# A layer kernel on one core: the inverse root of the gated norm moves from VectorE (a seed and three Newton steps) to one GpSimd power

## The chip, the cores and the metric

The kernel runs on one core of one Trainium2 chip. The metric is the device time of one launch in microseconds (us); the median of several runs counts. In the text TensorE is also called PE, VectorE DVE, ScalarE ACT, GpSimd POOL and SyncE SP, as the profile does.

## The reference

`x` is 4 x 512 x 256, that is 16 tiles of 128 tokens. Cut to what matters:

```
xn = (x - mean) / sqrt(var + 1e-5)
q, k, v = silu(xn Wq), silu(xn Wk), silu(xn Wv)         # 16 heads of 16
o  = chunked linear attention with decay, a state per head carried from chunk to chunk
o  = o * sigmoid((xn Wg1) Wg2)
og = o.reshape(b, n, 16, 16)
og = og * rsqrt(mean(og * og, axis=-1) + 1e-5)          # one factor per token and head
s  = (og * norm_w) Wo
g  = silu(quantised(xn) @ quantised(W2))                # through float8
out = x + s * g
```

The line with `rsqrt` is what the change touches: for one tile it is a table of 128 tokens x 16 heads.

## The kernel before

The program is written out by hand, with a semaphore for nearly every buffer. Each engine runs the same software pipeline over the 16 tiles: a step (i, j) works on tile n = 4i + j, prepares tile n+1 (projections, transposes) and tile n+2 (layer norm), finishes the norm and the transposed output of tile n-1, and the output projection and the sum with x of tile n-2. Steps 0 and 1 stand alone, steps 2 to 13 are a loop of three rounds with four steps in each, and steps 14 to 17 stand alone again: 16 has no tile n of its own any more, 17 only closes. Each engine takes its instructions in the order in which the program has them, so the order in `step` of each engine sets everything.

The parts that the change and the prediction touch, by engine:

- DVE: `gate_o` (L747) makes `og` = (tanh + 1) * o, which is twice the gated o; ACT `square_o` (L566) squares it; `sum_heads` (L753) sums 16 values of each head into `og_sum`, 128 x 16. `rsqrt` (L766 to L776) then makes `og_rs` in twelve small steps on 128 x 16, each of which waits for the one before over the semaphore `s_rs`: variance, shift right by one, seed from the constant 0x5F3759DF, and three times the three Newton instructions. In `step` they are spread by `newton(a, b)` between the other work of the engine.
- POOL: `norm_factor` (L336, L338) adds epsilon and takes the power -0.5 of a 128 x 1 column for the layer norm; `round_y` (L345, L348) and `put_nan` (L354) belong to the quantisation; `spread_state` (L375) writes the masked state, once or twice in a step; `add_x` (L392) makes `y` of tile n-2; `decay_k` (L361) makes `kd` of tile n+1; `head_norm` (L384) makes `on` = og * og_rs of tile n-1.
- PE: `transpose_o` (L1172) transposes `on`; it stands in the row just ahead of `add_chunk` (L1160), which completes `ps_o` of tile n, from which the next `gate_o` reads. `gate` (L1067) of the next step waits until `og` is made.
- DVE at a step's end: `decay_q` (L740), `exponent` (L688, which waits for ACT `e_y`, L561), `magic` (L692), `gate_o` (L747), `low_oT` (L782).
- The last tiles: in step 15 there is no tile to prepare, in step 16 `head_norm_last` on DVE (L793) takes the place of POOL's `head_norm`, and PE fills its wait with six matmul pairs of `keep_warm` (L1187).

Of the kernel before, what the change touches and what calls it, by code (L numbers as in the profile page):

```python
# [8 lines left out]
I32 = mybir.dt.int32  # L9
# [8 lines left out]
def layer_kernel(nc, x, log_decay, Wq, Wk, Wv, Wo, Wg1, Wg2, norm_w, W2, scale, scale1, out):  # L18
# [25 lines left out]
    LOOPS = B - 1  # L44
    RS_STEPS = 12
    WO_LOADS = 16 * (1 + KH)
# [6 lines left out]
    with ExitStack() as ctx:  # L53
# [90 lines left out]
        og_rs = sb("og_rs", [P, H])  # L144
        og_y2 = sb("og_y2", [P, H])
        og_half = sb("og_half", [P, H])
        on = sb("on", [P, D])
# [180 lines left out]
        def _(pool):  # L328
# [36 lines left out]
            def spread_state(i, j, c):  # L365


                if j % NB == NB - 1 and c == 1:
# [9 lines left out]
                                ALU.mult).then_inc(s_sx, 1)  # L378

            def head_norm(i, j):  # L380

                pool.wait_ge(s_rs, RS_STEPS * (num(i, j) + 1))
                need(pool, s_oTps, num(i, j))
                g.tensor_tensor(on[:].rearrange("p (h e) -> p h e", h=H), og[:].rearrange("p (h e) -> p h e", h=H),  # L384
                                og_rs[:].unsqueeze(2).broadcast_to([P, H, E]), ALU.mult).then_inc(s_on, 1)
# [64 lines left out]
            def step(pool, i, j):  # L450
# [10 lines left out]
                if cur:  # L461
                    spread_state(i, j, 0)

                if known(i, j - 2) and known(i, j - 1):
# [188 lines left out]
        def _(dve):  # L653
# [100 lines left out]

            def rsqrt(i, j, first, last):

                for m in range(first, last):
                    if m == 0:  # L760
                        dve.wait_ge(s_sum, num(i, j) + 1)
                        need(dve, s_on, num(i, j))
                    else:
                        dve.wait_ge(s_rs, RS_STEPS * num(i, j) + m)
                    if m == 0:
                        ins = v.tensor_scalar(og_var[:], og_sum[:], 1.0 / E, 4.0 * EPS, ALU.mult, ALU.add)  # L766
                    elif m == 1:
                        ins = v.tensor_scalar(og_half[:].bitcast(I32), og_var[:].bitcast(I32), 1, None, ALU.logical_shift_right)
                    elif m == 2:
                        ins = v.tensor_scalar(og_rs[:].bitcast(I32), og_half[:].bitcast(I32), -1.0, float(0x5F3759DF), ALU.mult, ALU.add)  # L770
                    elif m % 3 == 0:
                        ins = v.tensor_tensor(og_y2[:], og_rs[:], og_rs[:], ALU.mult)  # L772
                    elif m % 3 == 1:
                        ins = v.scalar_tensor_tensor(out=og_half[:], in0=og_y2[:], scalar=-0.5, in1=og_var[:], op0=ALU.mult, op1=ALU.mult)  # L774
                    else:
                        ins = v.scalar_tensor_tensor(out=og_rs[:], in0=og_half[:], scalar=1.5, in1=og_rs[:], op0=ALU.add, op1=ALU.mult)  # L776
                    ins.then_inc(s_rs, 1)

# [113 lines left out]
            def step(dve, i, j):  # L892
# [3 lines left out]

                def newton(a0, b0):
                    if back:
                        rsqrt(i, j - 1, a0, b0)

                if not cur:

                    if back:
                        sum_heads(i, j - 1)
                        newton(0, 8)
                    else:
                        dve.wait_ge(s_y, G - 1)
                    product(i, j - 2)
                    if back:
                        newton(8, RS_STEPS)  # L910
                        head_norm_last(i, j - 1)
                        low_oT(i, j - 1)
                    else:
                        add_x_last(i, j - 2)
                    return
                if not nxt:

                    mask(i, j, 0)
                    mask(i, j, 1)
                    add_state(i, j, 0)  # L920
                    mask(i, j, 2)
                    mask(i, j, 3)
                    sum_heads(i, j - 1)
                    newton(0, 2)
                    product(i, j - 2)
                    newton(2, RS_STEPS)
                    gate_o(i, j)
                    low_oT(i, j - 1)
                    return
# [14 lines left out]
                if first:  # L944
# [4 lines left out]
                    finish_w2()  # L949
                newton(0, 1)  # L950
                if nxt:
                    find_nan(i, j + 1)
                newton(1, 2)
                if known(i, j - 2):
                    product(i, j - 2)
                newton(2, 4)
                if norm and not first:
                    shift_x(i, j + 2)
                newton(4, 5)
                if cur and not first:  # L960
                    add_state(i, j, 0)
                newton(5, 6)
                if first:
                    scale_wo()
                if cur:
                    mask(i, j, 2)
                newton(6, 8)
                if cur:
                    mask(i, j, 3)
                newton(8, 9)  # L970
                if cur:
                    add_state(i, j, 1)
                newton(9, 10)
                if nxt:
                    low_g1(i, j + 1)
                newton(10, RS_STEPS)
                if norm:
# [317 lines left out]
```

## Time and profile before

| | us |
|---|---|
| median of three runs | 188.94 (188.51 to 189.07) |
| the profiled execution: its own time | 189.03 |
| its span, first to last instruction | 187.1 |
| PE busy | 166.7 (89% of the span) |
| DVE busy | 147.3 (79%) |
| POOL busy | 104.6 (56%) |
| ACT busy | 103.1 (55%) |

The profile is of one execution. The span leaves out 1.9 us at the edges of the execution. Busy times of the engines lie beside each other; which of them sets the end is read from the chain of waits, not from the shares. Rows of the trace give a start in us from the beginning of the span, a duration and the instruction, as out<-in; the shape is partitions x columns.

### The profile page before, as it was taken

The numbers are of one execution on the slowest core, as the hardware profiler recorded it, in microseconds if no ns is written. First come the engines' busy times: TensorE is split into PE (matmuls) and PEld (weight loads), VectorE is DVE, ScalarE is ACT, GpSimd is POOL, SyncE is SP. The second block draws the span as 40 slices with busy tenths as digits, with TensorE's granted clock in tenths as the row PEclk, the third lists the DMA queues.
The fourth block names the chain that finished last, engine by engine and source line by source line (L and its number), as shares of the span: only waits on it lengthen the run. The fifth ranks groups of instructions, "written<-read, shape, count | busy, mean of one in ns | idle before, by whom it ended". The sixth has DMA issues, their size and how long they took to land.

```text
span 187.1 us, 7410 instructions
## 1 busy us (share of the span) xinstructions
PE 166.7 (89%) x2510; PEld 127.1 (68%) x2510; DVE 147.3 (79%) x548; ACT 103.1 (55%) x283; POOL 104.6 (56%) x180
## 2 busy tenths in 40 slices
PE   4868469999999999999999999999999999998392
PEld 4745248677777777777777777777777777776181
DVE  1789985979797979888888879797979697857672
ACT  3584446483839383847575665748483847372100
POOL 6654871747565666656574656575747474732210
PEclk9999966999999999999999999999999999999657
DMA  5295300000100010000000000000000000010000
GB/s 145 71 254 166 112 5 0 4 4 4 33 0 32 0 33 4 30 4 28 0 28 0 28 0 27 1 0 28 0 28 0 28 0 28 0 33 4 28 28 28
DMA packets 7201, 5.82 MB, mean 31 GB/s; under 512 B 1744, under 2 KB 7184, under 8 KB 7184
## 3 DMA queue, kind: packets, MB, share of 16 engines
q1 hardware_dynamic: 7184, 5.60, 9.9%
q8 instruction: 10, 0.16, 0.4%
q14 instruction: 7, 0.06, 0.1%
HBM read 3.50 MB, written 2.10 MB: 30 GB/s over the span
## 4 chain that ended last, share of the span: by engine, by line
PE 61%; DVE 12%; ACT 11%; issue 8%; POOL 3%; DMA 3%; SPq 1%; ACTq 0%; DVEq 0%; POOLq 0%
PE b_scores L1081 11%; PE b_xo L1180 8%; PE b_att L1107 5%; PE b_kv L1028 4%; PE b_kv L1033 3%; PE b_kv L1030 3%; PE b_qg L1028 3%; ACT qT L526 3%; PE b_scores L1124 3%; PE b_gate L1067 3%; ACT ffn_silu L509 2%; DVE og L747 2%; ACT e_y L561 2%; PE b_att L1143 2%; PE b_qg L1033 2%
## 5 line engine op out<-in xcount | busy, mean ns | idle before, releaser
L1081 PE MATMUL b_scores<-qT,kT 32*64 32x128 f32 x512 | 31.6, 283 | 1.5 <-DVE probs L717 1.2
L717 DVE TENSOR_TENSOR probs<-b_scores,decay_mask 128x256 f32<-128x256 f32 x64 | 26.6, 418 | 2.6 <-PE b_scores L1081 2.3
L1081 PEld LDWEIGHTS b_scores<-qT,kT 32*64 32x64 f32 x512 | 20.1, 132 | 12.2 <-issue 8.9
L545 ACT ACTIVATE xn<-x_sb,shift,rstd 128x256 f32 (+1 forms) x15 | 9.0, 602 | 35.1 <-DVE shift L681 35.1
L375 POOL TENSOR_TENSOR state_c<-state,own_head 128x256 f32<-128x256 f32 x28 | 20.7, 738 | 11.3 <-DVE state L733 10.2
L345 POOL TENSOR_TENSOR e_sum<-e_y,e_magic 128x256 f32<-128x256 f32 x16 | 11.7, 729 | 25.0 <-DVE e_magic L692 25.0
L384 POOL TENSOR_TENSOR on<-og,og_rs 128x256 f32<-128x256 f32 x15 | 9.3, 622 | 17.3 <-DVE og_rs L776 15.5
L774 DVE SCALAR_TENSOR_TENSOR og_half<-og_y,og_var 128x16 f32<-128x16 f32 x48 | 14.7, 306 | 0.7
L392 POOL TENSOR_TENSOR y<-sg,x_sb 128x256 f32<-128x256 f32 x15 | 11.0, 731 | 6.1 <-DVE sg L787 6.1
L772 DVE TENSOR_TENSOR og_y<-og_rs 128x16 f32<-128x16 f32 x48 | 13.7, 285 | 0.8
L1124 PE MATMUL b_scores<-probs,v_parity 64*32 64x64 f32 x1024 | 14.0, 229 | 0.2 <-DVE probs L717 0.2
L1124 PEld LDWEIGHTS b_scores<-probs,v_parity 64*32 64x32 f32 x1024 | 11.4, 108 | 3.8 <-issue 3.3
L526 ACT ACTIVATE qT<-b_qk,head_parity 128x256 f32<-128x256 f32 x32 | 13.4, 474 | 0.0
L740 DVE TENSOR_TENSOR qdT<-b_qk,q_decay 128x256 f32<-128x256 f32 x16 | 6.8, 424 | 8.2 <-ACT qT L526 8.2
L1107 PE MATMUL b_att<-kv,kd 64*64 64x64 f32 x224 | 12.8, 234 | 0.0
L348 POOL TENSOR_TENSOR e_q<-e_sum,e_magic 128x256 bf16<-128x256 f32 x16 | 12.1, 754 | 1.3
L681 DVE SCALAR_TENSOR_TENSOR shift<-mean_var,rstd 128x1 f32<-128x1 f32 x16 | 10.5, 658 | 1.8 <-POOL rstd L338 0.8
L733 DVE SCALAR_TENSOR_TENSOR state<-state,chunk_decay,b_att 128x64 f32<-128x64 f32 x48 | 11.2, 273 | 0.9 <-issue 0.5
L688 DVE TENSOR_SCALAR e_exp<-e_y 128x256 int32<-128x256 int32 x16 | 4.7, 292 | 9.1 <-ACT e_y L561 9.1
L1107 PEld LDWEIGHTS b_att<-kv,kd 64*64 64x64 f32 x224 | 8.9, 136 | 4.3 <-issue 2.2
L354 POOL TENSOR_TENSOR xq<-e_q,e_nan 128x256 bf16<-128x256 bf16 x16 | 10.8, 674 | 1.7 <-DVE e_nan L698 1.7
L1187 PE MATMUL b_scores<-ident 128*128 128x128 f32 x46 | 9.5, 386 | 2.5 <-POOL ident L403 2.5
(135 smaller groups left out, 458.7 us busy)
## 6 DMA issues: line engine op xcount, KB each, us to landing
out_dram<-y SPq DMA_DIRECT2D x16, 128.0 KB, 1.7
x_sb<-in_L_attn_x_dram SPq DMA_DIRECT2D x3, 512.0 KB, 3.5
x_sb<-in_L_attn_x_dram SPq DMA_DIRECT2D x1, 384.0 KB, 5.4
w_f<-in_L_attn_Wk_dram SPq DMA_DIRECT2D x1, 256.0 KB, 2.9
w_f<-in_L_attn_Wv_dram SPq DMA_DIRECT2D x1, 256.0 KB, 3.1
w_f<-in_L_attn_Wq_dram SPq DMA_DIRECT2D x1, 256.0 KB, 3.4
w_f<-in_L_ffn_input_dram SPq DMA_DIRECT2D x1, 256.0 KB, 4.1
wo_f<-in_L_attn_Wo_dram SPq DMA_DIRECT2D x1, 256.0 KB, 3.9
```

The costliest lines, as they stand in the source:

```text
L345: g.tensor_tensor(e4_sum[:], e4_y[:], e4_magic[:], ALU.add).then_inc(s_e4p, 1)
L348: g.tensor_tensor(e4_q[:], e4_sum[:], e4_magic[:], ALU.subtract).then_inc(s_e4p, 1)
L375: g.tensor_tensor(dst[:].rearrange("p k (b c) -> p k b c", b=2), state[:].unsqueeze(2).broadcast_to([P, KH, 2, C]), own_head[:].rearrange( ...
L526: a.activation(qT[:, u, :, par, :], ps_qT, ACT.Copy, scale=head_parity[:, par:par + 1]).then_inc(s_qkT, 1)
L717: v.tensor_tensor(probs[:, r], b_score[r % 2][:, 0:4 * C].rearrange("p (i c) -> p i c", i=4), decay_mask[:, r], ALU.mult).then_inc(s_probs, 1)
L772: ins = v.tensor_tensor(og_y2[:], og_rs[:], og_rs[:], ALU.mult)
L774: ins = v.scalar_tensor_tensor(out=og_half[:], in0=og_y2[:], scalar=-0.5, in1=og_var[:], op0=ALU.mult, op1=ALU.mult)
L1028: t.matmul(dst, xT_hi[:, kk], w_hi[:, kk, a:b], start=(kk == 0), stop=False)
L1081: mm = t.matmul(b_score[r % 2][c * C:c * C + C, half * 2 * C:(half + 1) * 2 * C], kT[rows, u, half, c * C:c * C + C], qT[rows, u, half, :, ...
L1107: mm = t.matmul(ps_state[b * C:b * C + C, half, :], kd[rows, u, cols], kv[rows, u, D + cols.start:D + cols.stop], start=True, stop=True)
L1124: mm = t.matmul(ps_avT[32 * r:32 * r + 32, half, c, :], v_parity[rows, u, par * D + half * P + 32 * r:par * D + half * P + 32 * r + 32], p ...
L1180: mm = t.matmul(ps_out, lhs[:, kk], rhs[:, kk], start=(n == 0 and kk == 0), stop=(n == 2 and kk == KH - 1))
```

## The change

`rsqrt` goes. What is left of it on DVE is `head_var`, the first of the twelve instructions (variance, scaled and with epsilon). POOL gets `head_rsqrt`: one `tensor_tensor` with the operation power, variance to the exponent -0.5, on 128 x 16, with its result in `og_rs`. It stands behind the first `spread_state` of the step and ahead of `add_x`. In step 16, where `head_norm_last` runs on DVE, the power is on POOL all the same. The semaphore `s_rs` counts two steps for each tile in place of twelve.

```diff
@@ -42,7 +42,7 @@
     Q0 = 2 * D
     NW = 3 * D + GR
     LOOPS = B - 1
-    RS_STEPS = 12
+    RS_STEPS = 2
     WO_LOADS = 16 * (1 + KH)
     assert (P, NB, KH, HH, E, GR) == (128, 4, 2, 8, 16, 16)
 
@@ -142,8 +142,6 @@
         og_sum = sb("og_sum", [P, H])
         og_var = sb("og_var", [P, H])
         og_rs = sb("og_rs", [P, H])
-        og_y2 = sb("og_y2", [P, H])
-        og_half = sb("og_half", [P, H])
         on = sb("on", [P, D])
         oT_hi = sb("oT_hi", [P, KH, P], F32R)
         oT_lo = sb("oT_lo", [P, KH, P], F32R)
@@ -377,6 +375,11 @@
                                 own_head[:].rearrange("p (b c) -> p b c", b=2).unsqueeze(1).broadcast_to([P, KH, 2, C]),
                                 ALU.mult).then_inc(s_sx, 1)
 
+            def head_rsqrt(i, j):
+                pool.wait_ge(s_rs, RS_STEPS * num(i, j) + 1)
+                need(pool, s_on, num(i, j))
+                g.tensor_tensor(og_rs[:], og_var[:], minus_half[:], ALU.pow).then_inc(s_rs, 1)
+
             def head_norm(i, j):
 
                 pool.wait_ge(s_rs, RS_STEPS * (num(i, j) + 1))
@@ -460,7 +463,8 @@
                     put_nan(i, j + 1)
                 if cur:
                     spread_state(i, j, 0)
-
+                if known(i, j - 1):
+                    head_rsqrt(i, j - 1)
                 if known(i, j - 2) and known(i, j - 1):
                     add_x(i, j - 2)
                 if nxt:
@@ -752,29 +756,10 @@
                 need(dve, s_rs, RS_STEPS * num(i, j))
                 v.tensor_reduce(og_sum[:], og_sq[:].rearrange("p (h e) -> p h e", h=H), AX_X, ALU.add).then_inc(s_sum, 1)
 
-            def rsqrt(i, j, first, last):
-
-
-
-                for m in range(first, last):
-                    if m == 0:
-                        dve.wait_ge(s_sum, num(i, j) + 1)
-                        need(dve, s_on, num(i, j))
-                    else:
-                        dve.wait_ge(s_rs, RS_STEPS * num(i, j) + m)
-                    if m == 0:
-                        ins = v.tensor_scalar(og_var[:], og_sum[:], 1.0 / E, 4.0 * EPS, ALU.mult, ALU.add)
-                    elif m == 1:
-                        ins = v.tensor_scalar(og_half[:].bitcast(I32), og_var[:].bitcast(I32), 1, None, ALU.logical_shift_right)
-                    elif m == 2:
-                        ins = v.tensor_scalar(og_rs[:].bitcast(I32), og_half[:].bitcast(I32), -1.0, float(0x5F3759DF), ALU.mult, ALU.add)
-                    elif m % 3 == 0:
-                        ins = v.tensor_tensor(og_y2[:], og_rs[:], og_rs[:], ALU.mult)
-                    elif m % 3 == 1:
-                        ins = v.scalar_tensor_tensor(out=og_half[:], in0=og_y2[:], scalar=-0.5, in1=og_var[:], op0=ALU.mult, op1=ALU.mult)
-                    else:
-                        ins = v.scalar_tensor_tensor(out=og_rs[:], in0=og_half[:], scalar=1.5, in1=og_rs[:], op0=ALU.add, op1=ALU.mult)
-                    ins.then_inc(s_rs, 1)
+            def head_var(i, j):
+
+                dve.wait_ge(s_sum, num(i, j) + 1)
+                v.tensor_scalar(og_var[:], og_sum[:], 1.0 / E, 4.0 * EPS, ALU.mult, ALU.add).then_inc(s_rs, 1)
 
             def low_oT(i, j):
                 dve.wait_ge(s_oThi, num(i, j) + 1)
@@ -894,20 +879,15 @@
                 back = known(i, j - 1)
                 first = isinstance(i, int) and num(i, j) == 0
 
-                def newton(a0, b0):
-                    if back:
-                        rsqrt(i, j - 1, a0, b0)
-
                 if not cur:
 
                     if back:
                         sum_heads(i, j - 1)
-                        newton(0, 8)
+                        head_var(i, j - 1)
                     else:
                         dve.wait_ge(s_y, G - 1)
                     product(i, j - 2)
                     if back:
-                        newton(8, RS_STEPS)
                         head_norm_last(i, j - 1)
                         low_oT(i, j - 1)
                     else:
@@ -921,9 +901,8 @@
                     mask(i, j, 2)
                     mask(i, j, 3)
                     sum_heads(i, j - 1)
-                    newton(0, 2)
+                    head_var(i, j - 1)
                     product(i, j - 2)
-                    newton(2, RS_STEPS)
                     gate_o(i, j)
                     low_oT(i, j - 1)
                     return
@@ -947,33 +926,26 @@
                     magic(0, 1)
                     add_state(0, 0, 0)
                     finish_w2()
-                newton(0, 1)
+                if back:
+                    head_var(i, j - 1)
                 if nxt:
                     find_nan(i, j + 1)
-                newton(1, 2)
                 if known(i, j - 2):
                     product(i, j - 2)
-                newton(2, 4)
                 if norm and not first:
                     shift_x(i, j + 2)
-                newton(4, 5)
                 if cur and not first:
                     add_state(i, j, 0)
-                newton(5, 6)
                 if first:
                     scale_wo()
                 if cur:
                     mask(i, j, 2)
-                newton(6, 8)
                 if cur:
                     mask(i, j, 3)
-                newton(8, 9)
                 if cur:
                     add_state(i, j, 1)
-                newton(9, 10)
                 if nxt:
                     low_g1(i, j + 1)
-                newton(10, RS_STEPS)
                 if norm:
                     low_xT(i, j + 2)
                 if first:
```

What it does to the order on VectorE, from the variance of tile n-1 (`og_var`) to the first update of the state, in a step of the loop. Before:

```order
L766 TENSOR_SCALAR og_var<-og_sum 128x16
L696 REGISTER_ALU
L698 TENSOR_SCALAR e_nan<-e_q 128x256
L764 REGISTER_ALU
L768 TENSOR_SCALAR og_half<-og_var 128x16
L787 TENSOR_TENSOR sg<-b_xo,ffn_silu 128x256
L764 REGISTER_ALU
L770 TENSOR_SCALAR og_rs<-og_half 128x16
L764 REGISTER_ALU
L772 TENSOR_TENSOR og_y<-og_rs 128x16
L681 SCALAR_TENSOR_TENSOR shift<-mean_var,rstd 128x1
L764 REGISTER_ALU
```

and now, up to the update of the state:

```order
L762 TENSOR_SCALAR og_var<-og_sum 128x16
L700 REGISTER_ALU
L702 TENSOR_SCALAR e_nan<-e_q 128x256
L772 TENSOR_TENSOR sg<-b_xo,ffn_silu 128x256
L685 SCALAR_TENSOR_TENSOR shift<-mean_var,rstd 128x1
L728 ISA
L734 ISA
L737 SCALAR_TENSOR_TENSOR state<-state,chunk_decay,b_att 128x64 x2
```

The variance keeps its place; all that belonged to the seed and to the Newton steps is gone, here and further down the step.

On GpSimd, from the quantised x of tile n+1 (`xq`) over the spread state (`state_c`) to the normed output of tile n-1 (`on`), in the same step. Before:

```order
L354 TENSOR_TENSOR xq<-e_q,e_nan 128x256
L371 ISA
L375 TENSOR_TENSOR state_c<-state,own_head 128x256
L388 REGISTER_ALU
L390 ISA
L392 ISA
L392 TENSOR_TENSOR y<-sg,x_sb 128x256
L361 TENSOR_TENSOR kd<-kv,k_decay 128x256
L382 REGISTER_ALU
L384 TENSOR_TENSOR on<-og,og_rs 128x256
```

and now:

```order
L352 TENSOR_TENSOR xq<-e_q,e_nan 128x256
L369 ISA
L373 TENSOR_TENSOR state_c<-state,own_head 128x256
L379 ISA
L381 TENSOR_TENSOR og_rs<-og_var,minus_half 128x16
L393 ISA
L395 ISA
L395 TENSOR_TENSOR y<-sg,x_sb 128x256
L359 TENSOR_TENSOR kd<-kv,k_decay 128x256
L385 REGISTER_ALU
L387 TENSOR_TENSOR on<-og,og_rs 128x256
```

One instruction more stands between `state_c` and `y`, and `y`, `kd` and `on` all stand behind it.

## Rows read from the trace of the kernel before

**Rows 1.** The page's slices: TensorE's granted clock, 40 equal slices, in tenths

```profile
PEclk9999966999999999999999999999999999999657
```

**Rows 2.** Two steps: length, busy us of PE, PEld, DVE, ACT, POOL, granted clock

```profile
51.69:61.10 9.41, 9.18 (x157) 6.99 (x152) 7.96 (x32) 6.03 (x17) 5.48 (x9) 1.00 0.05 16
80.77:90.56 9.79, 9.79 (x170) 7.54 (x169) 8.31 (x34) 6.02 (x17) 6.16 (x10) 1.00 0.04 13
```

**Rows 3.** Waits over the whole span; us in total, times, longest

```profile
POOL on L384 <- DVE og_rs L776: 15.5, 14, 1.6
```

**Rows 4.** The chain of waits at a step's end; start us, us, what

```profile
89.53 0.41 ACT e_y L561
...
89.95 0.30 DVE e_exp L688
...
90.56 0.43 DVE og L747
...
91.08 0.36 PE b_gate L1067
```

**Rows 5.** Timeline of GpSimd in that step; start us, us, instruction, idle before

```profile
85.08 0.74 POOL L375 TENSOR_TENSOR state_c<-state,own_head 128x256 f32<-128x256 f32 x1 [0.56 <-DVE state L733]
85.78 0.73 POOL L392 TENSOR_TENSOR y<-sg,x_sb 128x256 f32<-128x256 f32 x1
86.46 0.63 POOL L361 TENSOR_TENSOR kd<-kv,k_decay 128x256 f32<-128x256 f32 x1
88.08 0.62 POOL L384 TENSOR_TENSOR on<-og,og_rs 128x256 f32<-128x256 f32 x1 [0.99 <-DVE og_rs L776]
88.66 0.74 POOL L375 TENSOR_TENSOR state_c<-state,own_head 128x256 f32<-128x256 f32 x1
```

**Rows 6.** Lines L338 (power) and L336 (sum) of GpSimd; durations ns min/median/max

```profile
L338 POOL TENSOR_TENSOR rstd<-var_eps,minus_half x16: 550/552/836, 3.9 to 151.2; 128x1 f32<-128x1 f32 x16
...
L336 POOL TENSOR_TENSOR var_eps<-mean_var,eps_col x16: 191/192/372, 3.6 to 150.9; 128x1 f32<-128x1 f32 x16
```

**Rows 7.** Groups of VectorE that the change removes; busy us, mean ns, idle before

```profile
L774 DVE SCALAR_TENSOR_TENSOR og_half<-og_y,og_var 128x16 f32<-128x16 f32 x48 | 14.7, 306 | 0.7
L772 DVE TENSOR_TENSOR og_y<-og_rs 128x16 f32<-128x16 f32 x48 | 13.7, 285 | 0.8
L776 DVE SCALAR_TENSOR_TENSOR og_rs<-og_half,og_rs 128x16 f32<-128x16 f32 x48 | 9.0, 188 | 0.7
L768 DVE TENSOR_SCALAR og_half<-og_var 128x16 int32<-128x16 int32 x16 | 3.1, 191 | 0.1
L770 DVE TENSOR_SCALAR og_rs<-og_half 128x16 int32<-128x16 int32 x16 | 2.7, 166 | 0.1
```

**Rows 8.** Timeline of TensorE at the end of that step

```profile
89.25 0.44 PE L1172 MATMUL b_xo<-ident,on 128*128 128x128 f32 x2
89.52 0.61 PE L1160 MATMUL b_att<-ident,avT 128*128 128x128 f32 x4
```

**Rows 9.** Timeline of VectorE at that step's start

```profile
80.77 0.41 DVE L747 SCALAR_TENSOR_TENSOR og<-gate_tanh,b_att 128x256 f32<-128x256 f32 x1
```

**Rows 10.** Timeline of all engines in step 15, tile 14's norm

```profile
171.94 0.17 DVE L766 TENSOR_SCALAR og_var<-og_sum 128x16 f32<-128x16 f32 x1
...
172.73 0.72 POOL L392 TENSOR_TENSOR y<-sg,x_sb 128x256 f32<-128x256 f32 x1 [2.11 <-DVE sg L787]
172.77 0.72 DVE L772 TENSOR_TENSOR og_y<-og_rs 128x16 f32<-128x16 f32 x1
...
172.96 0.71 PE L1160 MATMUL b_att<-ident,avT 128*128 128x128 f32 x4 [0.47 <-ACT avT L571]
...
174.98 0.17 DVE L776 SCALAR_TENSOR_TENSOR og_rs<-og_half,og_rs 128x16 f32<-128x16 f32 x1
175.23 0.62 POOL L384 TENSOR_TENSOR on<-og,og_rs 128x256 f32<-128x256 f32 x1 [1.78 <-DMA out_dram<-y]
...
175.91 0.69 PE L1172 MATMUL b_xo<-ident,on 128*128 128x128 f32 x2 [2.23 <-POOL on L384]
```

## Prediction

> **What bounds the kernel now.** I read in this order: the busy times by stretch, the chain of waits, the timeline of each engine over one step, the waits in total, and then the last steps alone.
>
> The windows show two steps of the loop, each from one `gate_o` to the next: 9.79 us where the state is updated twice, 9.41 us in every fourth step, where it is updated once [rows 2]. PE is busy for 9.79 of 9.79 and 9.18 of 9.41 us, DVE for 8.31, POOL for 6.16. The granted clock is 1.00, the upper of the two levels, 2.4 GHz. So PE is all but full. The chain shows what closes the loop beside it: ACT makes `e_y`, DVE `e_exp`, the magic number and `og`, and then PE goes on with the gate matmul L1067 [rows 4]. `e_exp` starts when `e_y` is there, so DVE stands idle ahead of it however little it had to do before. None of the Newton instructions is in that chain. They end in `og_rs`, for which POOL's `on` waits, 14 times, 15.5 us in all [rows 3]; but `on` ends at 88.70 [rows 5] and PE takes it at 89.25, behind other matmuls [rows 8]. That wait is POOL's and costs nothing as long as `on` is there by then.
>
> **What is removed.** 176 instructions on DVE: three groups of 48 with 14.7, 13.7 and 9.0 us, and two of 16 with 3.1 and 2.7 us, together 43.2 us of busy time, 2.7 us for each of 16 tiles [rows 7]. In the loop I cost this at nothing: what DVE hands to PE and ACT next hangs on `e_y` [rows 4], and PE is full [rows 2]. What comes instead when it goes is a longer idle time ahead of `e_exp`.
>
> **What is added.** 16 powers of 128 x 16 on POOL, one for a tile. They stand ahead of `y`, `kd` and `on` of the same step, so each of these is later by the length D of the power, less the wait of `on`, which now follows `kd` at once.
>
> D is in no row. The nearest is the power of 128 x 1, 552 ns, and beside it the sum of 128 x 1, 192 ns [rows 6]. `y`, a sum of 128 x 256, takes 0.73 us [rows 5], so a column of a plain operation costs (730 - 192) / 255 = 2.1 ns. The power of one column costs 360 ns more than its sum. If all of this is paid once an instruction, D = 552 + 15 x 2 = 0.58 us. If it is paid again for each column, D = 192 + 16 x 360 = 5.95 us. The two ends are a factor of ten apart. Halfway by ratio is 1.86 us, halfway by difference 3.3 us. The row that D is nearest to is the 128 x 1 power itself, and it stands at the lower end, so I take little above the ratio's middle: 2.1 us, which is 0.10 us for each further column, under a third of the 0.36 us.
>
> The Trainium skill (GPSIMD Engine Reference, Performance pitfalls for Q7 kernels) says that a chain of dependent fp32 operations on these cores pays 4 cycles an operation unless independent work is interleaved. The 360 ns for one column agree with a long chain of that sort; by the rule without interleaving D is at its upper end, with it near the lower, and no row of the trace tells which. The sum would be that of the second or of the first rival below.
>
> **What D does to a step.** I lay the power into the step from 80.77 to 90.56. `state_c` starts at 85.08, and the power takes the place of `y` at 85.78 [rows 5]. Then `y` starts at 85.78 + D, `kd` 0.68 us later, `on` 0.65 us after that, at 87.11 + D, and it ends at 87.73 + D. PE wants it at 89.25 [rows 8], so up to D = 1.5 us nothing is late.
>
> Behind that, two loops form, and the longer sets the step:
> - `og` 80.77 [rows 9], then `on` at 87.73 + D, the transpose L1172 0.04 us later, L1160 0.27 us after it, 0.61 us long [rows 8], and the next `og` 0.05 us later, at 88.70 + D. The step is 7.93 + D. It passes 9.79 at D = 1.86 and 9.41 at D = 1.48.
> - In steps with two updates the second `state_c` starts 0.58 us after `on` starts and takes 0.74 us [rows 5]: it ends at 88.43 + D. If `e_exp` can't run beside it, the next `og` comes 0.61 us later [rows 4], at 89.04 + D, and the step is 8.27 + D, longer than 9.79 from D = 1.52.
>
> Whether the second loop is real hangs on one thing. In step 15 the Newton product `og_y` on 128 x 16 took 0.72 us, from 172.77 to the end of POOL's `y` [rows 10], while its group has a mean of 285 ns [rows 7]: DVE stood still while POOL ran. I take the mean of both loops. The Trainium skill (SBUF — State Buffer, SBUF: two separate sides) says that GpSimd and VectorE share one pair of ports as a lock held for a whole instruction, and that a VectorE operation with two inputs from SBUF, or in a two-port mode, waits for it; the rows on `og_y` agree. By it the power keeps such instructions off for all of D, and the second loop is the one that counts.
>
> With D = 2.1 us the loops give 10.03 and 10.37 us. For the ten steps of tiles 2 to 14 with two updates that is 0.24 to 0.58 us over 9.79, mean 0.41, so 4.1 us; for the three with one update 10.03 - 9.41 = 0.62, so 1.9 us. Step 1 has no `y` ahead of `on` and stays. Together +6.0 us.
>
> **The end.** In step 15 nothing else covers the Newton steps. `og_var` of tile 14 ends at 172.11, the last Newton step at 175.15, and `on` starts at 175.23; PE waits for it for 2.23 us, though it was free from 173.67 on [rows 10]. Afterwards the power runs at about 172.15, `y` behind it for 0.69 us, and `on` starts at 172.84 + D: earlier by 2.39 - D, with D = 2.1 by 0.3 us. In step 16 the power is beside the matmuls of `keep_warm`, which I cost at nothing; it costs what D is longer than the eleven Newton instructions that it replaces there.
>
> **Sum.** 189.03 + 6.0 - 0.3 = 194.7 us for an execution like the profiled one. That is 0.09 above the median before, which gives 194.6; I say 194.7.
>
> **The rivals.**
> - *The power is cheap* (D from 0.58 to 1.5 us). For it: every other POOL instruction grows by only 2.1 ns a column. Against it: the power is the one whose first column costs 360 ns. Nothing is late in the loop, and the end gains 2.39 - D: with D = 1.0 us 1.4 us, so 187.5 us; from 1.8 to 0.9 us over the case. If the shorter wait also keeps the clock up, of which the page shows 0.6, 0.5 and 0.7 in the last three slices [rows 1], it is up to 1.5 us more. This is the case on the other side. It decides below D = 1.5 us, and its price is only the end.
> - *The power is paid in full for each column* (D from 3.6 to 5.95 us). With D = 4.0 the loops give 11.93 and 12.27: 10 x 2.31 + 3 x 2.52 = 30.7, and 1.6 later at the end, so 221 us; with 5.95 about 249. Against it: sixteen columns would have to share nothing. PE would then stand idle for over 2 us in each step, and after the 2.23 us wait in step 15 the clock fell [rows 1, 10], which would add to it.
> - *The relief of VectorE counts* after all: 2.7 us a tile less on an engine that is busy for 8.31 of 9.79 us. Against it stands the idle time that already lies ahead of `e_exp`. The only gap on PE is 0.23 us, in the steps of 9.41 us [rows 2], so at most 3 x 0.23 = 0.7 us and the end: 186.9 us.
>
> **Chances.** Middle power, D from 1.5 to 3.6 us, own range 189 (D = 1.6) to 215 us: 0.44, and the forecast 194.7. Full price: 0.18. Cheap: 0.34. Relief: 0.04. A difference under 0.3%, 0.57 us, is what a measurement of this kernel can't tell; it takes in D from about 1.55 to 1.7 us and the cheap case's upper edge, 0.08. So faster 0.35, same 0.08, slower 0.57. The range from 187.0 to 222 leaves out D above 4.1 us and the best of the cheap case.
>
> **What would show it.** The duration of `og_rs` on POOL is the first number to read. If D is near 2.1 us, PE shows a wait ahead of L1172 for `on` of some tenths of a us in nearly every step, the steps are 10.0 to 10.4 us long, and `on` follows `kd` without idle time. If D is under 1.5 us, the steps stay at 9.79 and 9.41, DVE's idle time ahead of `e_exp` grows, and the only change is ahead of L1172 in step 15. The forecast is wrong if D is outside 1.5 to 3.6 us, or if the steps don't follow 7.93 + D to 8.27 + D. If `e_exp` starts with the end of the second `state_c`, the second loop is right; if the two overlap, the first.

## The result, and the profile after

| | before | after |
|---|---|---|
| median, us | 188.72 (188.14 to 189.07, 4 runs) | 203.94 (203.36 to 204.63, 4 runs) |
| span of the profiled execution, us | 187.1 | 202.9 |
| PE busy, us (share) | 166.7 (89%) | 171.2 (84%) |
| DVE busy | 147.3 (79%) | 123.3 (61%) |
| POOL busy | 104.6 (56%) | 150.6 (74%) |

The ratio is 1.078 (95% interval 1.0737 to 1.0823): 15 us slower, forecast 6 us slower. DVE lost 24 us of busy time and POOL gained 46 us. The 43.2 us of the removed groups [rows 7] shrink to 24 mainly because their records partly overlap those of DVE's other work (with each stretch counted once they fill 28.5 us alone), and because `e_exp` and the magic number take 5.4 us more in all.

Two groups of the page after, and its slices of the clock (columns: busy us, mean ns | idle before, releaser):

```profile
L381 POOL TENSOR_TENSOR og_rs<-og_var,minus_half 128x16 f32<-128x16 f32 x16 | 46.7, 2917 | 3.8 <-DVE og_var L762 3.8
L1144 PE MATMUL b_xo<-ident,on 128*128 128x128 f32 x32 | 7.3, 310 | 15.3 <-POOL on L387 15.0
...
PEclk9999756999999999999699999999999969999757
```

The power takes 2.92 us, not 2.1. PE now waits for `on` ahead of its transposes, 15.0 us in all; before, it did so only at the end. The slices of the clock dip twice within the loop as well, where before [rows 1] those of the loop all stood at 9.

The waits say the same from both sides; `on`, for which POOL waited 15.5 us before [rows 3], now never waits:

```profile
PE b_xo L1144 <- POOL on L387: 15.0, 12, 2.8
...
DVE on L778 <- POOL og_rs L381: 1.4, 1, 1.4
```

Two steps of the loop, from one `gate_o` to the next (the columns of [rows 2]):

```profile
86.32:97.07 10.75, 9.61 (x157) 7.33 (x156) 7.24 (x22) 6.13 (x17) 9.06 (x12) 1.00 0.04 13
97.07:108.19 11.12, 11.12 (x163) 8.77 (x164) 5.84 (x21) 6.41 (x18) 8.29 (x10) 0.85 0.03 12
```

Where [rows 2] had 9.79 us with PE busy throughout, there are 10.75 us with 9.61 busy. In the second step the clock was on its lower level from 98.4 to about 101.8; PE had been busy since 96.15, the end of a wait of 1.14 us.

The same step on POOL and PE, to be laid beside [rows 5] and [rows 8]:

```profile
90.61 0.74 POOL L373 TENSOR_TENSOR state_c<-state,own_head 128x256 f32<-128x256 f32 x1 [0.47 <-DVE state L737]
91.31 2.92 POOL L381 TENSOR_TENSOR og_rs<-og_var,minus_half 128x16 f32<-128x16 f32 x1
94.20 0.73 POOL L395 TENSOR_TENSOR y<-sg,x_sb 128x256 f32<-128x256 f32 x1
94.89 0.62 POOL L359 TENSOR_TENSOR kd<-kv,k_decay 128x256 f32<-128x256 f32 x1
95.47 0.62 POOL L387 TENSOR_TENSOR on<-og,og_rs 128x256 f32<-128x256 f32 x1
...
96.15 0.44 PE L1144 MATMUL b_xo<-ident,on 128*128 128x128 f32 x2 [1.14 <-POOL on L387]
```

From `state_c` to the end of `on` POOL works without a gap, and PE starts 0.06 us after `on` ends.

Where the 15.8 us of span went, by the starts of `og` in the two timelines: the start of tile 0 is later by 0.17; from tile 0 to 1 the step grew from 9.02 to 10.38, 1.36; from tile 1 to 14 from 126.13 to 139.51, 13.38; from tile 14 to the end from 19.13 to 20.02, 0.89.

### The profile page after: what moved, and what is told of

Read it like the earlier page. It is cut to its first block, busy times and chain, and to the rows that moved or that the text cites. A ratio compares the mean times of both kernels' runs of the same rounds, so it can differ in the third digit from the quotient of the medians.

```text
span 202.9 us, 7112 instructions
## 1 busy us (share of the span) xinstructions
PE 171.2 (84%) x2510; PEld 130.3 (64%) x2510; DVE 123.3 (61%) x372; ACT 104.2 (51%) x283; POOL 150.6 (74%) x196
## 4 chain that ended last, share of the span: by engine, by line
issue 32%; PE 19%; POOL 18%; DVE 6%; ACT 3%; POOLq 1%; DVEq 1%; ACTq 0%
POOL og_rs L381 4%; POOL xq L352 4%; POOL on L387 4%; PE b_scores L1053 3%; POOL kd L359 3%; PE b_xo L1144 3%; PE b_xo L1152 2%; PE b_att L1132 2%; POOL y L395 2%; DVE og L751 1%; POOL state_c L373 1%; DVE probs L721 1%; PE b_kv L1002 1%; PE b_kv L1000 1%; POOL var_eps L334 1%
## 5 line engine op out<-in xcount | busy, mean ns | idle before, releaser
L381 POOL TENSOR_TENSOR og_rs<-og_var,minus_half 128x16 f32<-128x16 f32 x16 | 46.7, 2917 | 3.8 <-DVE og_var L762 3.8
L1053 PE MATMUL b_scores<-qT,kT 32*64 32x128 f32 x512 | 31.7, 283 | 1.1 <-DVE probs L721 1.1
L343 POOL TENSOR_TENSOR e_sum<-e_y,e_magic 128x256 f32<-128x256 f32 x16 | 11.6, 728 | 11.7 <-DVE e_magic L696 11.7
L1144 PE MATMUL b_xo<-ident,on 128*128 128x128 f32 x32 | 7.3, 310 | 15.3 <-POOL on L387 15.0
L541 ACT ACTIVATE oT_hi<-b_xo 128x256 fp32r<-128x256 f32 x16 | 6.2, 386 | 20.5 <-PE b_xo L1144 20.5
L1144 PEld LDWEIGHTS b_xo<-ident,on 128*128 128x128 f32 x32 | 3.3, 145 | 19.0 <-POOL on L387 18.3
L334 POOL TENSOR_TENSOR var_eps<-mean_var,eps_col 128x1 f32<-128x1 f32 x16 | 3.2, 203 | 15.1 <-DVE mean_var L677 15.1
L685 DVE SCALAR_TENSOR_TENSOR shift<-mean_var,rstd 128x1 f32<-128x1 f32 x16 | 9.5, 592 | 6.0 <-POOL rstd L336 3.3
L1000 PE MATMUL b_kv<-w_hi,xT_hi 128*128 128x512 f32 x32 | 11.1, 431 | 1.8 <-ACT xT_hi L488 1.8
L692 DVE TENSOR_SCALAR e_exp<-e_y 128x256 int32<-128x256 int32 x16 | 6.4, 403 | 9.1 <-ACT e_y L565 9.1
```

Of the source, the lines that this page charges most:

```text
L343: g.tensor_tensor(e4_sum[:], e4_y[:], e4_magic[:], ALU.add).then_inc(s_e4p, 1)
L381: g.tensor_tensor(og_rs[:], og_var[:], minus_half[:], ALU.pow).then_inc(s_rs, 1)
L1000: t.matmul(dst, xT_hi[:, kk], w_hi[:, kk, a:b], start=(kk == 0), stop=False)
L1053: mm = t.matmul(b_score[r % 2][c * C:c * C + C, half * 2 * C:(half + 1) * 2 * C], kT[rows, u, half, c * C:c * C + C], qT[rows, u, half, :, ...
L1144: mm = t.transpose(ps_oT[:, kk, :], on[:, kk * P:kk * P + P], ident[:])
```

## The experiments

**e1: what a power costs.** `for w in (1, 2, 4, 8, 16, 32, 64): tensor_tensor(out, base[:, 0:w], exponent[:, 0:w], pow)` (shortened), two further powers of 16 columns (bases of 1.0; 16 partitions only) and two products, behind GpSimd's last work in the kernel before.

> The kernel before, with a row of GpSimd operations put behind its last one: powers -0.5 of 1, 2, 4, 8, 16, 32 and 64 columns on 128 partitions, then 16 columns with all bases 1.0, 16 columns on 16 partitions only, and as a yardstick plain products of 16 and 64 columns. Its time isn't the question (a few us longer), the durations are. Theory (the power pays per column beyond its first): from 0.55 us for one column and 2.92 for sixteen, (2.92 - 0.55)/15 = 0.158 us a column, so 0.71, 1.02, 1.66, 2.92, 5.4 and 10.5 us. Rival A (the 2.92 us in the changed kernel are mostly a wait for a port that VectorE holds): here VectorE is idle or nearly so, and sixteen columns take well under 2.9 us. Rival B (cost in blocks, a fixed price up to 16 columns): 2 to 16 columns all near 2.9 us. If bases of 1.0 are quicker the data decide, and if 16 partitions are quicker the cores' number of lanes does; the theory expects the same 2.92 us for both.

Groups of POOL with shapes kept apart (columns as in [rows 7]):

```profile
L481 POOL TENSOR_TENSOR sweep_out<-lag_decay,sweep_exp 128x64 f32<-128x64 f32 x1 | 10.5, 10542 | 0.0
L481 POOL TENSOR_TENSOR sweep_out<-lag_decay,sweep_exp 128x32 f32<-128x32 f32 x1 | 5.4, 5422 | 0.0
L481 POOL TENSOR_TENSOR sweep_out<-lag_decay,sweep_exp 128x16 f32<-128x16 f32 x1 | 2.9, 2896 | 0.0
L483 POOL TENSOR_TENSOR sweep_out<-ones_row,sweep_exp 128x16 f32<-128x16 f32 x1 | 2.9, 2895 | 0.0
L485 POOL TENSOR_TENSOR sweep_out<-lag_decay,sweep_exp 16x16 f32<-16x16 f32 x1 | 2.9, 2890 | 0.0
...
L481 POOL TENSOR_TENSOR sweep_out<-lag_decay,sweep_exp 128x8 f32<-128x8 f32 x1 | 1.6, 1632 | 0.0
...
L481 POOL TENSOR_TENSOR sweep_out<-lag_decay,sweep_exp 128x4 f32<-128x4 f32 x1 | 1.0, 1009 | 0.0
...
L481 POOL TENSOR_TENSOR sweep_out<-lag_decay,sweep_exp 128x2 f32<-128x2 f32 x1 | 0.7, 733 | 0.0
L481 POOL TENSOR_TENSOR sweep_out<-lag_decay,sweep_exp 128x1 f32<-128x1 f32 x1 | 0.5, 549 | 0.1
...
L487 POOL TENSOR_TENSOR sweep_out<-lag_decay,sweep_exp 128x16 f32<-128x16 f32 x1 | 0.2, 210 | 0.0
```

The price is a straight line: (10542 - 549) / 63 = 159 ns a column, neither the 2 ns nor the 360 ns of the two bounds. Sixteen columns take the same with an idle VectorE (it had no work from 186.42 us on), with bases of 1.0 and on 16 partitions, and shorter powers are cheaper, so rivals A and B fall. The time, 212.22 us in the one run, is the added work.

**e2: a product in place of the power.**

```diff
-g.tensor_tensor(og_rs[:], og_var[:], minus_half[:], ALU.pow)
+g.tensor_tensor(og_rs[:], og_var[:], minus_half[:], ALU.mult)
```

> The changed kernel with a product in place of the power, in the same place and shape (this leaves the inverse root out of the result). D falls from 2.92 to about 0.22 us. Theory (only the length of the power on the way to `on` costs): steps back at 9.79 and 9.41 us, and step 15 earlier by 2.39 - 0.22 = 2.2 us, so 186.6 us. Rival (VectorE's relief itself is worth something, or costs something by a changed order): 185.5 or less, or no gain at 188.7.

186.23 us, ratio 0.9846 (0.9777 to 0.9916). The 13 steps from tile 1 to 14 take 126.20 us against 126.13 before, so the relief of VectorE, here 32 us of busy time (115.0 against 147.3), is worth nothing in the loop; the gain is at the end, from `og` of tile 14 on 16.35 us against 19.13. A slowdown by the changed order, apart from D, is excluded. The median gain is 2.7 us, and its interval, 1.6 to 4.2 us, holds the 2.2 expected (the 186.6 us were a hit). In the trace step 15 is shorter by 1.98 us, from 8.02 to 6.04, against 2.39 - 0.22 = 2.17 by the prediction's formula; what made the other 0.8 us, behind step 15, stays open.

**e3: the power on 8 columns, e10: on 11 columns.** The slices `[:, 0:8]` and `[:, 0:11]` of all three operands; the other heads keep a factor of 1.

> The changed kernel with the power on 8 of the 16 columns only (the other eight heads keep a factor of 1, so half of the inverse roots are left out). If a column costs 0.158 us, D = 1.66 us. Theory of the first loop (a step is 7.93 + D): 9.59 us, so nothing over 9.79 in the two-update steps, 0.2 us in each of three others, and 2.39 - 1.66 = 0.7 us won in step 15: 188.5 us. With the second loop (8.27 + D = 9.93) it would be 1.4 us more, 189.9. Rival (a fixed price for up to 16 columns): 203 us or more.

> The changed kernel with the power on 11 of the 16 columns (the other five heads keep a factor of 1, so these inverse roots are left out). By 0.158 us a column D is 2.11 us, the value that the forecast took. Theory (only the size of D was wrong, the way from D to the time was right): the steps are 7.93 + 2.11 = 10.04 us by the first loop, also the three that were 9.41, and 10.38 by the second; the sum of the forecast, 194.7 us against 188.9 to 189.0 before, plus 0.3 us for step 1, which the forecast left out, so 194 to 195.5, or 192.5 if only the first loop counts. Rival (there is a further cost, which the forecast didn't have): over 197 us.

| columns | power, us | time, us | ratio (95%) | steps with two updates | with one |
|---|---|---|---|---|---|
| 8 | 1.65 | 188.18 | 0.9958 (0.9924 to 0.9992) | 9.81 to 9.93 | 9.43 to 9.46 |
| 11 | 2.13 | 192.24 | 1.0152 (1.0124 to 1.0181) | 9.95 to 10.10 | 9.82 to 9.88 |
| 16 | 2.92 | 203.94 | 1.078 (1.0737 to 1.0823) | 10.59 to 10.81 | 10.73 to 10.77 |

(Without the two steps of 11.12 and 11.62 us in which the clock fell; rows for tiles 2 to 13.) With 8 columns the first loop gives 9.58 us: less than the 9.79 of the steps with two updates, and in the three steps with one update PE waits for `on` for 0.23 to 0.29 us. The time expected was 188.5 us. With 11 columns the step is 7.93 + 2.13 = 10.06 in the first loop and 10.40 in the second: measured is the first. With 16 it is 10.85. So the first loop holds at three lengths within 0.3 us. The expectation for e10 of 194 to 195.5 us, which took in the second loop, failed; its 192.5 for the first loop alone holds.

**e4: the Newton steps kept, and a power beside them.** In the kernel before, `g.tensor_tensor(spare_rs[:], k_decay[:], minus_half[:], ALU.pow)` behind the first `spread_state`.

> The kernel before with all its Newton steps on VectorE, and in addition a power of 128 x 16 on GpSimd in the place where the changed kernel has its own; its result goes to a spare tile. Theory (the power's place and length on GpSimd cost, and nothing comes from VectorE): the loop as in the changed kernel, 13 to 14.5 us longer than before; in step 15 the power can run early, since it doesn't wait for the variance: 202 us. Rival (the removal of the Newton steps and the new wait of the power on the variance make up part of the loss): 195 us or less.

205.57 us, ratio 1.087 (1.0827 to 1.0914). The whole loss is there though nothing was taken from VectorE and nobody reads the power. The expected 202 were too few: most steps took 10.7 to 10.9 us, but the clock fell in three, and they took 11.74 and 11.75 us, and 11.24 in tile 14.

**e8: matmuls for nothing ahead of PE's wait.**

```diff
+for _ in range(3):
+    t.matmul(b_xo[:, 0:P], ident[:], ident[:], start=True, stop=True)
 pe.wait_ge(s_on, num(i, j) + 1)
```

(Shortened: not in the last tile, and the wait for `xT_lo` now stands ahead of the three.)

> The changed kernel, and PE runs three matmuls of 128 x 128 for nothing ahead of its wait for `on`, into the bank that the transposes then overwrite: 0.7 of the 1.1 us for which it waits there. Theory (the two steps of the changed kernel in which the granted clock fell, 11.12 and 11.62 us in place of 10.75, come from PE's repeated idle time): the clock stays up in the loop, all steps are 10.6 to 10.8 us, 1.3 us less, 202.6 us. Rival (these falls have another cause, or the fillers delay the transposes): 204 us or more.

204.40 us, ratio 1.0821 (1.0761 to 1.0881). The expected 202.6 were missed. In its profile all steps of tiles 2 to 13 take 10.64 to 10.79 us and the clock stays up in the loop. But tile 14 takes 10.35 us, where it took 9.57 in the changed kernel, directly behind the second fall of the clock: most of what that fall had cost came back in the next step. From tile 1 to 14 it is 138.95 against 139.51 us, and the median of all runs isn't lower than the 203.94. That the idle time lets the clock fall fits this one profile; a gain in time is not shown.

**e9: does the power keep the port?** Four powers of 32 columns behind the end, a VectorE operation just behind the start of each.

> The kernel before, and behind its end four powers of 32 columns (5.4 us each) on GpSimd, with one VectorE operation sent off just as each of them begins: a product of PSUM and SBUF, a product of two SBUF tensors, a product with a constant on 128 x 256, and one on a single column. The durations are the question. Theory (a power keeps the common port for all of its time, as other GpSimd operations do): the PSUM product takes its usual 0.42 us and the single column its usual 0.15 to 0.2 us, the product of two SBUF tensors and the 128 x 256 with a constant end with the power, about 5 us after they were sent. Rival (the power reads 32 columns in a moment and computes for the rest, so the port is free): all four take their usual 0.17 to 0.42 us.

VectorE in the timeline; the powers ran from 186.68, 192.55, 198.41 and 204.26, 5.43 to 5.44 us each:

```profile
186.75 0.42 DVE L1018 TENSOR_TENSOR port_psum<-b_xo,port_a 128x256 f32<-128x256 f32 x1 [0.41 <-POOL port_out L491]
...
192.62 0.46 DVE L1022 TENSOR_TENSOR port_two<-port_a 128x256 f32<-128x256 f32 x1 [0.32 <-POOL port_out L491]
...
198.49 0.32 DVE L1026 TENSOR_SCALAR port_one<-port_a 128x256 f32<-128x256 f32 x1 [0.32 <-POOL port_out L491]
...
204.34 0.16 DVE L1030 TENSOR_SCALAR port_bf<-port_a 128x1 bf16<-128x1 f32 x1 [0.31 <-POOL port_out L491]
```

All four took about their usual time (a product from PSUM 0.42, `y` on two SBUF tensors 0.42, `e_exp` with a constant 0.29 us). The theory, that a power holds the port for all of its length, is wrong; the rival holds for an operation that comes 0.07 us behind the power's start.

For later ones the trace of e4 has the answer, since there the Newton steps run beside the power, `og_y` with both inputs from SBUF:

```profile
91.08 0.50 DVE L776 TENSOR_TENSOR og_y<-og_rs 128x16 f32<-128x16 f32 x1
...
91.52 2.91 POOL L467 TENSOR_TENSOR spare_rs<-k_decay,minus_half 128x16 f32<-128x16 f32 x1
...
93.15 0.17 DVE L776 TENSOR_TENSOR og_y<-og_rs 128x16 f32<-128x16 f32 x1
```

The first stood beside `state_c` and ended with it. Sixteen `og_y` began 0.62 to 2.65 us behind a power's start and ended within it; each took 0.17 or 0.18 us, and so did 26 `og_rs`, which read two different tensors, 0.54 to 2.72 us behind the start.

**e5, e6, e7, e11: other places for the power.** The order of a step on POOL, from `xq` on:

```
changed kernel:  xq  state_c  POWER  y        kd  on  state_c
e5:              xq  state_c  POWER  on       y   kd  state_c
e6:              xq  POWER    state_c  on     y   kd  state_c
e7:              xq  POWER    state_c  on     kd  state_c          (y on VectorE, behind low_g1)
e11:             xq  POWER    state_c  on     kd  state_c  y       (VectorE: xT_lo ahead of the second state update)
```

> The changed kernel with `on` directly behind the power on GpSimd, ahead of `y` and `kd` (and a wait of VectorE for `y` in step 16, since the order no longer covers it). `on` ends 1.37 us earlier in the step, at 86.41 + D on the clock of the step from 80.77. Theory (PE's wait for `on` sets the step): the first loop is 6.56 + D = 9.5 us, under 9.79. What is next is GpSimd itself: 10.6 us from `og` to the end of the second `state_c`, which then meets the next step's `e_sum`, `e_q` and `var_eps`, so 9.9 to 10.1 us a step, and 191 to 193 us in all. Rival (GpSimd's total busy time of some 9 us a step is what costs, wherever the power stands): 10.7 us a step as in the changed kernel, 203 us.

197.16 us, ratio 1.0443 (1.0398 to 1.0489), where I expected 191 to 193. In the loop PE hardly waits for `on` any more (0.34 to 0.39 us in the steps with one update), but the steps with two updates are 10.35 to 10.59 us, 0.5 us over what I expected, and those with one 9.86 to 9.90: now `og` is late, and PE waits 6.1 us for it in all. VectorE at the end of such a step:

```profile
93.76 0.74 DVE L692 TENSOR_SCALAR e_exp<-e_y 128x256 int32<-128x256 int32 x1 [0.61 <-ACT e_y L565]
94.61 0.62 DVE L696 TENSOR_SCALAR e_magic<-e_exp 128x256 f32<-128x256 f32 x1
95.16 0.41 DVE L751 SCALAR_TENSOR_TENSOR og<-gate_tanh,b_att 128x256 f32<-128x256 f32 x1
```

`e_exp` and the magic number took 0.29 us each in e2 and take 0.74 and 0.62, each until 0.15 us after the end of a running operation of POOL, which by now works without a gap there (`kd` from 93.74 for 0.62 us, `state_c` from 94.31 for 0.77).

> As e5_on_first, but the power stands ahead of the first `state_c`, directly behind `xq`. The variance is there by then, so the power starts 0.56 + 0.70 us earlier and fills the time in which GpSimd waited for the state. Theory: `on` is in time by over a us, GpSimd has 9.06 us of work in a step and 0.6 us of waiting for `mean_var`, so it is just about full: 9.8 to 9.95 us a step, 189 to 191 us. Rival (the delay of `state_c` by 1.7 us holds up PE's state matmuls or VectorE's second state update): 193 us or more.

198.23 us, ratio 1.0508 (1.0466 to 1.055): worse than e5, and the theory of 189 to 191 us fell. The loop itself is better than in e5, 130.72 us from tile 1 to 14 against 133.54, with 10.25 to 10.35 us for two updates and 9.58 for one. The end is worse, 24.06 us from tile 14 on against 19.46: step 15 takes 11.88 us, since the variance comes late there and the power, ahead of `state_c` in the row, holds back the state that PE needs for that same tile (PE stands for 5.1 us ahead of its matmul). POOL in step 15:

```profile
177.04 2.91 POOL L381 TENSOR_TENSOR og_rs<-og_var,minus_half 128x16 f32<-128x16 f32 x1 [4.83 <-DVE og_var L762]
179.92 0.72 POOL L373 TENSOR_TENSOR state_c<-state,own_head 128x256 f32<-128x256 f32 x1
```

> As e6_power_early, and in addition the sum of the product with x (`y`) moves from GpSimd to VectorE, behind the second mask, where VectorE now waits. GpSimd is down to 8.4 us a step. Theory: the steps are back at 9.79 and 9.41 us; in step 15 `on` no longer has `y` ahead of it, the power takes as long there as the Newton steps did, so no gain or loss at the end: 188 to 189 us, the same as before the change. Rival (the two engines hold each other up at their common port once GpSimd works almost without a gap): `e_exp`, the magic number and `y` on VectorE each wait for a GpSimd instruction, 10.1 us a step or more, 193 us.

198.61 us, ratio 1.0549 (1.0504 to 1.0595), steps of 10.14 to 10.42 us with two updates, 9.59 with one, and again 11.87 in step 15. The rival's step of 10.1 us or more came, not its total of 193 us, since it left out the loss in step 15. And it came mostly by another wait: VectorE's second state update waits for the late `state_c`, and `xT_lo`, for which PE waits, is queued behind it:

```profile
90.45 0.47 DVE L735 SCALAR_TENSOR_TENSOR state<-state,chunk_decay,b_att 128x64 f32<-128x64 f32 x2 [1.31 <-POOL state_c L373]
...
92.27 0.41 PE L1146 MATMUL b_xo<-ident,on 128*128 128x128 f32 x2 [0.63 <-DVE xT_lo L705]
```

> The power on all 16 columns, in the best order that the other runs suggest: the power directly behind `xq`, then `state_c`, `on`, `kd`, the second `state_c`, and `y` last; VectorE makes `xT_lo` ahead of the second state update, which waits for `state_c`; VectorE waits for `y` ahead of the next product and not ahead of the magic number; in step 15 the state goes ahead of the power again. Theory (in e6_power_early PE waited for `xT_lo` behind a state update, and the end lost 3.9 us by a power ahead of the state): PE has no wait for `on` or `xT_lo`, what is left is `e_exp` and the magic number beside GpSimd's last operations, 10.0 to 10.2 us a step, 193 to 195 us. Rival (GpSimd's 9.1 us of work a step, with its waits for `mean_var`, are the bound by now): 10.3 us a step, 197 us. In neither case is it faster than before the change.

193.63 us, ratio 1.0231 (1.0196 to 1.0267), as the theory said (193 to 195); steps of 10.18 to 10.29 us, and of 9.50 with one update. The steps with two updates are a little over the 10.0 to 10.2 expected. In the loop PE waits for neither `on` nor `xT_lo`. One thing is left: `y` on POOL, and `e_exp` beside it.

```profile
91.70 0.73 POOL L395 TENSOR_TENSOR y<-sg,x_sb 128x256 f32<-128x256 f32 x1
...
91.79 0.80 DVE L695 TENSOR_SCALAR e_exp<-e_y 128x256 int32<-128x256 int32 x1 [0.61 <-ACT e_y L568]
```

**e12: `y` into POOL's gap.** `round_y` of tile n+2 (`e_sum`, `e_q`) at the end of a step, and `add_x` behind it, where POOL waited for `mean_var`. Against e11 (shortened; the old `round_y` of tile n+1 at the start of the step goes):

```diff
 if cur:
     spread_state(i, j, 1)
+if norm:
+    round_y(i, j + 2)
 if known(i, j - 2) and known(i, j - 1):
     add_x(i, j - 2)
```

> As e11_all_orders, with `y` moved once more: GpSimd now makes `e_sum` and `e_q` of the next tile at the end of a step and `y` behind them, in the 0.5 us in which it waited for `mean_var`, so that no `y` of 0.7 us runs while VectorE wants to start `e_exp`. Theory (a VectorE operation on one or two SBUF tensors is held for the rest of a running GpSimd operation that streams its tensors, here `e_exp` by `y`, 0.5 us a step, and that is all that is left of the loss): `e_exp` takes 0.3 to 0.4 us, the steps are 9.8 to 9.95 us, everything on GpSimd is 0.2 us later than before and still in time, 188.5 to 190.5 us, so level with the kernel before or a little slower. Rival (GpSimd with 9.1 us of work in 9.8 us has no room, so `on` or the second `state_c` becomes late instead): 10.1 us a step or more, 193 us as e11.

189.89 us (12 runs) against 189.06 (17 runs), ratio 1.0045 (1.0023 to 1.0067), within the 188.5 to 190.5 expected.

```profile
82.64 0.74 POOL L395 TENSOR_TENSOR y<-sg,x_sb 128x256 f32<-128x256 f32 x1
83.35 0.25 POOL L334 TENSOR_TENSOR var_eps<-mean_var,eps_col 128x1 f32<-128x1 f32 x1
...
84.82 2.92 POOL L381 TENSOR_TENSOR og_rs<-og_var,minus_half 128x16 f32<-128x16 f32 x1
...
89.55 0.74 POOL L373 TENSOR_TENSOR state_c<-state,own_head 128x256 f32<-128x256 f32 x1
...
90.25 0.29 DVE L696 TENSOR_SCALAR e_exp<-e_y 128x256 int32<-128x256 int32 x1 [0.61 <-ACT e_y L569]
```

In the loop `e_exp` takes 0.29 us again, but for one of 0.44; the steps are 9.75 to 9.99 and 9.35 to 9.39 us. A power of the full 2.92 us in each step is now all but free: 14 of the 15 us are back by order alone, and the 0.8 us that are left are small, but clear of noise. No version that makes the whole norm is faster than the kernel before.

## Why the prediction was wrong, point by point

**The direction and the mechanism were right.** PE all but full, the Newton steps off the chain, `y`, `kd` and `on` pushed back by D, PE waiting ahead of L1144: rows, waits and e2, e3, e4 and e10 show each. e4 shows it most directly. The direction was in part luck: it hung on D alone, which no row gave, and with D = 1.65 us (e3) the kernel would not have become slower.

**The step that failed is the length of the power, D.** I took 0.10 us for each further column, 2.1 us in all; measured are 0.159 and 2.92 us. The bounds, 0.58 and 5.95 us, held it, and halfway by difference would have been 3.3, nearer than what I chose. Going below it because the 128 x 1 row "stands at the lower end" was no argument: one column shows the sum of the fixed and the repeated part, not how they divide. It mattered so much because D stood near the edge: between 11 and 16 columns 0.79 us more a power turned 192.24 into 203.94, 11.7 us over 14 steps.

**The first loop, 7.93 + D,** held (e3, e10). With 2.92 it gives 10.85 us a step; measured are 10.59 to 10.81. Put into the sum of the prediction, D = 2.92 gives 206.2 us with the mean of both loops and 204.5 with the first alone. That the latter is so near the measured 203.94 is again partly luck, since tile 14 is counted too high in it and step 1 is left out.

**The second loop, 8.27 + D,** did not. In the changed kernel `e_exp` got in between `on` and the second `state_c`: it took 0.59 and not 0.29 us and the magic number 0.63, to 96.98, and `og` at 97.07 started as soon as L1132 allowed it, at 97.03. So the path over DVE was as good as equally long, but no longer. By taking the mean of both loops I put in 0.17 us a step too much. The rule of the Trainium skill (SBUF — State Buffer, SBUF: two separate sides) that I named there, a lock for the whole instruction, fits the plain operations (0.80 us of `e_exp` beside `y` in e11), but not the power: e9 shows both kinds of VectorE operation at about full speed beside its start, and e4 the kind with two inputs up to 2.7 us behind it, and there the measurement decides.

**At the D that I assumed, the sum was too high.** With 11 columns, D = 2.13, the kernel takes 3.1 us more than before where I had 5.7 at D = 2.1. The second loop is 1.7 us of that; I had counted tile 14 as a step of 9.79, but it has no layer norm, took 9.46 before and 9.49 now; and the short steps became 9.82 to 9.88, not 10.03, for which no run shows the reason. So the two errors had opposite signs, and the one in D was the greater.

**Step 1** "stays", I said. It has 0.68 us less ahead of `on`, but with D = 2.92 that isn't enough: 9.02 became 10.38, and PE waits 1.06 us for `on` there; with 11 columns it waits 0.28 us, so the term was not nothing at the D of the forecast either. Not all of the 1.36 us is the power's. In the traces of e1 and e9, whose loop is that of the kernel before, step 1 took 9.54 and 9.46 us: there the lower clock of the start lasted to 33.7 and 33.1 us, and in the changed kernel to 33.5, where before it ended at 31.5. In e4, where it ended at 31.7, step 1 took 10.09, so 1.07 us more with nearly the same clock.

**The end.** In step 15 I had a gain of 2.39 - D: with 2.92 a loss of 0.5, and step 15 grew from 8.02 to 8.54. With 8 and 11 columns the formula gives gains of 0.7 and 0.3, and step 15 took 7.27 and 7.73. So it holds at each length. Another 0.4 were lost behind it. In step 16, which I costed at nothing, VectorE waits 1.39 us for the power; yet `on` starts 3.20 us behind the start of `og_var`, against 3.26 with the eleven Newton instructions. What is new is that `on` there takes 0.94 in place of 0.43 us, beside POOL's `y` (from 196.39 for 0.73), and that PE waits 0.29 us behind `keep_warm`.

**The clock** I had only for the case of waits over 2 us. It fell in two steps of the loop, after waits of PE of 1.14 and 0.85 us, though not after the two longest in the loop, 1.54 and 1.49. These steps took 1.2 us in all over neighbours of the same kind (11.12 against 10.77, 11.62 against 10.81), of which about 0.8 came back in tile 14 (9.57 us, against 10.35 in e8).

**The rivals.** The cheap power is excluded by e1. The full price is excluded by it too, though D lies nearer to its edge of 3.6 us than I liked. The relief of VectorE is worth nothing in the loop (e2).

## What to carry to other kernels

When an operation moves to an engine that is half idle, what counts is not its idle share but what is queued behind the place and when the first of these is wanted; write that down as slack (here 1.5 us) and compare the new operation with it. A price known for one column says nothing about sixteen: if both bounds are a factor of ten apart and the slack lies between them, the direction is a guess, and the middle by difference is no worse a guess than the middle by ratio. And a long operation can often be hidden after all: find the engine's own waits, and put into each of them the work that nobody waits for.

## What the runs showed of the hardware

- A GpSimd power to -0.5 costs 0.39 us and 0.159 us a column of fp32, against 210 ns for a product of 16 columns. Neither bases of 1.0 nor 16 partitions in place of 128 change it (e1, 2.90 and 2.89 us).
- It doesn't hold back VectorE operations on SBUF, neither just behind its start (e9: 0.46 and 0.32 us beside a power of 5.43 us) nor later (e4: `og_y` and `og_rs` of 0.17 to 0.18 us up to 2.7 us behind it), while a GpSimd sum of 128 x 256 does: `e_exp` took 0.80 in place of 0.29 us (e11, e12). In the loops of e5, e6 and e11 a stretched `e_exp` ended 0.14 to 0.16 us after the end of a GpSimd operation, be it `y`, `kd` or `state_c`.
- In the changed kernel the granted clock fell in two steps, after waits of PE of 1.14 and 0.85 us; after others of 0.89 to 1.54 us it did not.
